# Decay sums of a selective scan: float32 products with a triangle, or broadcast bfloat16 weights over the triangle with the key's side as a bias

## The reference

```
dt = clip(softplus(dt + dt_bias), 0.001, 0.1);  A = -exp(A_log)
dA = min(exp(dt * A), 0.99)
h_t = clip(dA_t * h_{t-1} + x_t B_t^T, -10, 10)      # per sequence and head, 64 x 64
y_t = C_t h_t
```

## Time and profile before

| | |
|---|---|
| median of the runs | 1929.37 us (1928.33 to 1934.06) |
| profiled execution | 1936.8 us, its span 1934.7 us |
| the scan, first to last L2136 | 1684.13 to 1804.17 us, 120.04 us |
| TensorE busy there | 118.03 us, granted clock 1.00 |
| VectorE, ScalarE, GpSimd busy there | 102.05, 87.89 and 0.00 us |
| from there to the feed-forward | 12.61 us, granted clock 0.51 |

### The profile page before, as it was taken

The page is one execution under the profiler, slowest core; times in us unless marked ns, Lnnn a source line. Parts: engine busy times, 40 slices in busy tenths (PEclk is TensorE's granted clock), DMA queues, the critical chain, the costliest instruction groups (busy, mean ns, idle before and its releaser), DMA issues.

```text
span 1934.7 us, 41332 instructions
## 1 busy us (share of the span) xinstructions
PE 1749.8 (90%) x15442; PEld 659.6 (34%) x15442; DVE 1642.7 (85%) x2549; ACT 1522.6 (79%) x2881; POOL 459.9 (24%) x751
## 2 busy tenths in 40 slices
PE   7699999999999999999999999998996688899884
PEld 4232222222222222222222222226772344366552
DVE  7689999999999999999999999943345776588678
ACT  6469999999999999999999999993333567777454
POOL 2233210230001223222223222000006775000024
PEclk9799999999999999999999999999997899899787
DMA  3412222111101111111111111015765453423311
GB/s 119 158 63 88 75 66 66 53 56 41 30 28 41 51 41 46 53 40 43 56 42 42 53 45 56 10 39 158 211 173 156 110 143 104 134 61 88 93 62 33
DMA packets 156350, 146.36 MB, mean 76 GB/s; under 512 B 39882, under 2 KB 135117, under 8 KB 156002
## 3 DMA queue, kind: packets, MB, share of 16 engines
q1 hardware_dynamic: 147688, 126.17, 22.1%
q0 software_dynamic: 8352, 17.29, 3.3%
q10 hardware_dynamic: 122, 0.39, 0.1%
HBM read 80.80 MB, written 60.03 MB: 73 GB/s over the span
## 4 chain that ended last, share of the span: by engine, by line
PE 73%; ACT 9%; POOL 6%; issue 5%; DVE 4%; DMA 2%; ACTq 0%; SPq 0%; POOLq 0%; DVEq 0%
PE PS L1870 28%; PE PS L1896 16%; PE PS L1854 10%; POOL VP L1728 6%; ACT probs L1263 4%; PE PS L1943 4%; ACT SG L1252 2%; PE PS L2138 2%; PE PS L2120 1%; PE PS L1930 1%; PE PS L1816 1%; PE PS L2210 1%; PE PS L2141 1%; PE PS L2123 1%; PE PS L1922 1%
## 5 line engine op out<-in xcount | busy, mean ns | idle before, releaser
L812 DVE TENSOR_REDUCE mxp<-PS 128x1 f32<-128x1024 f32 x1024 | 1171.9, 1214 | 34.9 <-PE PS L1854 31.3
L1263 ACT ACTIVATE probs<-PS 128x512 f32<-128x512 f32 x2048 | 1095.9, 596 | 59.3 <-PE PS L1896 11.5
L1870 PE MATMUL PS<-probs,VH 128*32 128x256 f32 x8192 | 655.5, 392 | 35.4 <-ACT probs L1263 21.2
L1896 PE MATMUL PS<-stacks 51*128 51x512 bf16 x2048 | 414.5, 387 | 2.1 <-DVE mxp L812 1.1
L1854 PE MATMUL PS<-stacks 48*128 48x512 bf16 x2048 | 403.9, 380 | 13.3 <-DMA stacks<-kl_d 12.8
L1870 PEld LDWEIGHTS PS<-probs,VH 128*32 128x32 f32 x8192 | 162.3, 108 | 468.6 <-ACT probs L1263 239.7
L1896 PEld LDWEIGHTS PS<-stacks 51*128 51x128 bf16 x2048 | 109.9, 93 | 427.3 <-ACT probs L1263 393.1
L1728 POOL DMA_INDIRECT VP<-oe_d,ROWI x128 | 134.1, 1048 | 217.7 <-DMA oe_d<-stacks 174.1
L1620 POOL DMA_INDIRECT xe_d<-xn_s,rows_s x128 | 126.4, 988 | 214.9 <-PE PS L1870 181.6
L1598 POOL CAST spl<-nmx 128x8 bf16<-128x8 f32 x64 | 12.0, 188 | 514.3 <-DVE nmx L807 300.9
L826 DVE TENSOR_TENSOR stacks<-stacks,PS 128x640 f32<-128x640 f32 x32 | 26.3, 821 | 112.6 <-ACT stacks L1304 112.6
(11 more groups left out here) (358 smaller groups left out, 1809.4 us busy)
## 6 DMA issues: line engine op xcount, KB each, us to landing
xe_d<-zt SPq DMA_DIRECT2D x16, 640.0 KB
stacks<-xe_d SPq DMA_DIRECT2D x32, 320.0 KB, 3.7
oe_d<-stacks SPq DMA_DIRECT2D x32, 320.0 KB, 2.8
o_d<-SG SPq DMA_DIRECT2D x256, 32.0 KB, 1.9
ews<-in_ew_dram SPq DMA_DIRECT2D x33, 192.0 KB, 2.4
stacks<-ql_d SPq DMA_DIRECT2D x64, 96.0 KB
stacks<-kl_d SPq DMA_DIRECT2D x62, 96.0 KB
probs<-xs_d SPq DMA_DIRECT2D x18, 256.0 KB, 3.7
```

What stands on the lines that cost most here:

```text
L812: v.tensor_reduce(mxp[:, n // 2, n % 2:n % 2 + 1], MXB[n % 2].rearrange("p a c -> p (a c)"), X_AX, ALU.max).then_inc(mx_done, 1)
L1263: act.activation(probs[:, at:at + 512], PS[:, bank_of(u, e), :], ACT.Exp, scale=float(1.0 / np.sqrt(np.float32(DK)))).then_inc(exp_done, 1)
L1870: mm = pe.matmul(OB[32 * jg:32 * jg + 32, c:c + 256], VH[w][:, kt, :], probs[:, at:at + 256], start=(kt < 2 and half == 0), stop=(kt >= TC ...
L1896: pe.matmul(PS[:, bank_of(u, e), :], KS[w][o:o + KROWS + 3, kt * P:(kt + 1) * P], QS[w][o:o + KROWS + 3, q0:q0 + 512], start=True, stop=Tr ...
```

## The change

The exponent of a pair is no longer computed as one sum over the tokens between s and t. The running sums are made on their own, and the two sides of the pair meet in the exponential.

The decays are cut into three bfloat16 numbers whose sum is the float32 value (`la3`, once, before the scan). For each pair and each of the three parts, TensorE takes one column of them, repeated 128 times with step 0, as 128x128 weights over the triangle in bfloat16: `L_t`, the same in all 128 partitions. The key's side, `-L_s`, is one number for each partition: three matmuls before the scan give it for all chunks (bank 7), and ScalarE adds it as the bias of the exponential, one instruction for each pair. Above the diagonal the exponent is then positive, so VectorE bounds it by 1 before it multiplies with the triangle. `E2` is read from the same two banks, so bank 7 isn't used in the loop.

GpSimd takes over the squares of x, the turned bfloat16 copy of `E2` (now from `E2`, not a second exponential) and that of `DM`. VectorE's `spread_decays` is gone; its product into `DM` now waits for GpSimd's copy of the last `DM`.

```
+        la3 = spare[:, 0:3 * NT * NH1 // 2].bitcast(BF16).rearrange("p (k t h) -> p k t h", k=3, h=NH1)
+        tri16 = spare[:, 256:256 + P // 2].bitcast(BF16)
...
             def chunk_operands(c):
                 w = c % 2
-                if c + 1 < TCH:
-                    spread_decays(c + 1)
                 v.wait_ge(d_done, c + 1)
-                v.tensor_tensor(DM, DE, TRI.unsqueeze(1).broadcast_to([P, B * NH1, P]), ALU.mult).then_inc(dm_done, 1)
+                after(v, opb_ready, c)
+                v.scalar_tensor_tensor(DM, DE, 1.0, TRI.unsqueeze(1).broadcast_to([P, B * NH1, P]), ALU.min, ALU.mult).then_inc(dm_done, 1)
...
-            spread_decays(0)
+            link(v.tensor_copy(tri16, TRI))
+            link(v.tensor_copy(la3[:, 0], d0))
+            link(v.tensor_tensor(la_rest, d0, la3[:, 0], ALU.subtract))
+            link(v.tensor_copy(la3[:, 1], la_rest))
+            v.tensor_tensor(la3[:, 2], la_rest, la3[:, 1], ALU.subtract).then_inc(la_set, 1)
...
+            v.wait_ge(la_ready, 1)
+            v.tensor_scalar(d2, PS[:, 7, 0:NT * NH1].rearrange("p (t h) -> p t h", h=NH1), -1.0, None, ALU.mult).then_inc(la_set, 1)
...
             def chunk_exps(c):
                 w = c % 2
-                act.wait_ge(la_ready, c + 1)
+                act.wait_ge(la_ready, c + 2)
                 after(act, ops_ready, c)
-                act.activation(DE, PS[:, 0:2, :].rearrange("p b (h t) -> p (b h) t", h=NH1), ACT.Exp).then_inc(d_done, 1)
+                for b in range(B):
+                    for h in range(NH1):
+                        ins = act.activation(DE[:, b * NH1 + h, :], PS[:, b, h * P:(h + 1) * P], ACT.Exp,
+                                             bias=dtt[:, 1, b * TCH + c, h:h + 1])
+                ins.then_inc(d_done, 1)
                 after(act, hs_done, c - 1)
-                sums = by_head(PS[:, 7, :])
-                act.activation(E2[w], sums, ACT.Exp)
-                act.activation(E2b[w][:, :, 1:P], sums[:, :, 0:P - 1], ACT.Exp)
-                act.activation(E2b[w][:, :, 0:1], sums[:, :, P - 1:P], ACT.Exp).then_inc(el_done, 1)
+                for b in range(B):
+                    ins = act.activation(E2[w][rows_of(b), :, :], by_head(PS[rows_of(b), b, :]), ACT.Exp)
+                ins.then_inc(el_done, 1)
                 act.wait_ge(tile_ld[c % 4], TILE_BASE + 96 * (c // 4 + 1))
-                act.activation(RB[w][:, :, :, 0:HP], XS[c % 4].rearrange("p (b h n) -> p b h n", b=B, h=NH1), ACT.Square)
                 for b in range(B):
-                    act.activation(RB[w][:, b, :, HP:P], BS[c % 4][:, b, :].unsqueeze(1).broadcast_to([P, NH1, DS]), ACT.Square)
-                act.wait_ge(dm_done, c + 1)
-                act.activation(DMb[w][:, :, 1:P], DM[:, :, 0:P - 1], ACT.Copy)
-                act.activation(DMb[w][:, :, 0:1], DM[:, :, P - 1:P], ACT.Copy).then_inc(opb_ready, 1)
+                    ins = act.activation(RB[w][:, b, :, HP:P], BS[c % 4][:, b, :].unsqueeze(1).broadcast_to([P, NH1, DS]), ACT.Square)
+                ins.then_inc(sq_done, 1)
...
+            for c in range(TCH):
+                w = c % 2
+                pool.wait_ge(tile_ld[c % 4], TILE_BASE + 96 * (c // 4 + 1))
+                after(pool, c_done, c - 1)
+                xs = XS[c % 4].rearrange("p (b h n) -> p b h n", b=B, h=NH1)
+                for b in range(B):
+                    pool.tensor_tensor(RB[w][:, b, :, 0:HP], xs[:, b], xs[:, b], ALU.mult)
+                pool.wait_ge(el_done, c + 1)
+                pool.tensor_copy(E2b[w][:, :, 1:P], E2[w][:, :, 0:P - 1])
+                pool.tensor_copy(E2b[w][:, :, 0:1], E2[w][:, :, P - 1:P])
+                pool.wait_ge(dm_done, c + 1)
+                pool.tensor_copy(DMb[w][:, :, 1:P], DM[:, :, 0:P - 1])
+                pool.tensor_copy(DMb[w][:, :, 0:1], DM[:, :, P - 1:P]).then_inc(opb_ready, 1)
...
             def chunk_sums(c):
-                pe.wait_ge(lb_set, c + 1)
-                after(pe, d_done, c)
-                scaled = lb.rearrange("p (b h) t -> p b (h t)", b=B)
-                for b in range(B):
-                    pe.matmul(PS[:, b, :], BELOW, scaled[:, b, :], start=True, stop=True)
                 after(pe, el_done, c)
                 for b in range(B):
-                    mm = pe.matmul(PS[rows_of(b), 7, :], onesq[:, 0:DS], scaled[:, b, :], start=True, stop=True)
+                    for h in range(NH1):
+                        for k in range(3):
+                            mm = pe.matmul(PS[:, b, h * P:(h + 1) * P], la3[:, k, b * TCH + c, h:h + 1].broadcast_to([P, P]), tri16,
+                                           start=(h == 0 and k == 0), stop=(h == NH1 - 1 and k == 2))
                 mm.then_inc(la_ready, 1)
...
                 pe.wait_ge(opb_ready, c + 1)
+                pe.wait_ge(sq_done, SQ_BASE + c + 1)
...
+            pe.wait_ge(la_set, 1)
+            for k in range(3):
+                mm = pe.matmul(PS[:, 7, 0:NT * NH1], tri16, la3[:, k].rearrange("p t h -> p (t h)"), start=(k == 0), stop=(k == 2))
+            mm.then_inc(la_ready, 1)
             chunk_sums(0)
```

More of the change, by code:

```diff
@@ L236, in build @@
         sc_aff = sb("sc_aff", [P, 3, DI])
-        lb, DE, DM, MM0 = (VP[:, 8 * i:8 * i + 8, :] for i in range(4))
+        DE, DM, MM0 = (VP[:, 8 * i:8 * i + 8, :] for i in range(1, 4))
+        spare = VP[:, 0:8, :].rearrange("p t c -> p (t c)")
+        la3 = spare[:, 0:3 * NT * NH1 // 2].bitcast(BF16).rearrange("p (k t h) -> p k t h", k=3, h=NH1)
+        tri16 = spare[:, 256:256 + P // 2].bitcast(BF16)
+        la_rest = spare[:, 512:512 + NT * NH1].rearrange("p (t h) -> p t h", h=NH1)
         MM = [MM0, YM[:, 0:8, :]]
@@ L250, in build @@
         BD = [heads(t) for t in (probs[:, 3072:3584], ym_flat[:, 2048:2560])]
-        ldc = sb("ldc", [P, B, NH1])
         HS = sb("HS", [P, NH1, HP])
@@ L337, in build @@
         tile_ld = [sem(f"tile_ld{i}") for i in range(4)]
-        lb_set, la_ready, gg_set, d_done, el_done, dm_done, opb_ready, vr_out, ops_ready, c_done, y_out, hs_done = (
-            sem(n) for n in ("lb_set", "la_ready", "gg_set", "d_done", "el_done", "dm_done", "opb_ready", "vr_out", "ops_ready", "c_done", "y_out", "hs_done"))
+        la_set, la_ready, gg_set, d_done, el_done, dm_done, opb_ready, vr_out, ops_ready, c_done, y_out, hs_done = (
+            sem(n) for n in ("la_set", "la_ready", "gg_set", "d_done", "el_done", "dm_done", "opb_ready", "vr_out", "ops_ready", "c_done", "y_out", "hs_done"))
         bnd_read, yc_ready = sem("bnd_read"), sem("yc_ready")
+        sq_done, SQ_BASE = exp_out, 4
         okv = sb("okv", [P, 1])
@@ L1480, in chunk_out @@
                     act.activation(VR[b * DS:b * DS + 1, :, :], PS[0:1, 5 + b, :].rearrange("p (h t) -> p h t", h=NH1), ACT.Copy).then_inc(vr_out, 1)
+            act.wait_ge(la_set, 2)
             chunk_exps(0)
```

## The result

The changed kernel takes 1938.55 us (median of 20 runs, 1931.72 to 1953.87); the kernel before, run beside it, 1931.57 us (20 runs). The ratio is 1.0045, interval [1.003, 1.006]: slower by 7 us in medians, where 13.5 us less were forecast. The profiled execution took 1943.99 us.

The account below looks back on a forecast made before the run. TensorE's 8.09 us a chunk was taken to bound the scan. Fifteen chunks at 7.1 us give 106.5 us against 120.0, so -13.5 us from the median of 1929.4: 1916 us, range 1909 to 1929.

Parts of the forecast that it names:

- The rule on the clock: TensorE in the scan: its clock falls only after idling 2 us and more; expected gaps are under 0.5 us.
- rival E: TensorE idles a little each period and its clock falls: 5.17 + 1.66 us double to 13.7 us; chance 0.02.
- The collision: In the scan, GpSimd's casts delay VectorE's two-SBUF-input work, chiefly L1015: 0.27 us taken, making 7.1 us a chunk.
- Start at 0, bound +2: First chunk: second sums may run at 1.2 GHz after TensorE idles 2.6 us, at most +2 us; 0 taken.
- Part 1: Sums on TensorE: 24 bfloat16 matmuls at 0.069 us, 1.66 us a chunk, replace 2.92 us.
- Rival C: Step-0 weights load slowly on TensorE: 0.121 us a matmul, 8.07 us a chunk, 1929 to 1930 us; chance 0.08.
- Part 2 and 3: ScalarE: eight exponentials for DE, 2.2 us, hidden behind TensorE; VectorE: no decay spread, product into DM 1.23 us.
- rival B: ScalarE's DE is late: 7.2 us a chunk without collisions, 7.7 with them; 1919 to 1925 us; chance 0.15.
- Part 4: GpSimd in the scan: squares and casts sum to 3.5 us a chunk, half the period, with exclusion against VectorE.
- rival D: GpSimd with the exclusion becomes the bound: 8.9 us a chunk with dear casts, 1941 us; chance 0.12.
- 6.83 us loop: Scan: TensorE's products, then VectorE's four operations renewing the state; sums can shrink 1.26 us before this ends last.
- Rival A: Nothing collides in the scan: 6.83 us a chunk, 102.5 us, kernel 1908 to 1912 us; chance 0.13.

Follow-up runs that it names:

- e1: Changed kernel plus 12 useless bfloat16 matmuls a chunk on TensorE, ahead of the wait for the new state: 1927.77 us, ratio to before 0.9978.
- e8: Changed kernel without GpSimd's part; squares of x, `E2b` and `DMb` on ScalarE as before: ratio to before 1.0093.
- e2: Changed kernel with GpSimd's squares of x held until VectorE has renewed the state two chunks before: 1917.9 us, ratio to before 0.9936.
- e3: Changed kernel with the squares of x back on ScalarE, so GpSimd only copies: 1920.3 us, ratio to before 0.9941.
- e7: Changed kernel with only 60 useless matmuls added before the second sums: ratio to before 1.0025.
- e12: Changed kernel plus 6 useless matmuls a chunk in TensorE's idle time: ratio to before 1.0004.
- e5: e2 plus 40 useless matmuls between first and second sums and an early exponential loading ScalarE's table: ratio to before 0.9956.
- e6: e5 plus the state's first product before VectorE's wait for `DE`, and 34 useless matmuls before the last chunk's products: ratio to before 0.9927.
- e10: e6 run again on another chip: ratio to before 0.9941.
- e11: Kernel before with only GpSimd's part of the change, plus 14 useless float32 matmuls around the second sums: ratio to before 1.0036.

## Why the prediction was wrong

The trace of before had a sign of it, outside the scan. First two rows of its windows, then TensorE between them, then the window behind:

```profile
1870.00:1878.00 8.00, 8.00 (x33) 4.10 (x32) 7.40 (x32) 4.41 (x9) 0.00 (x0) 1.00 0.01 3
1878.00:1880.00 2.00, 1.42 (x11) 1.23 (x11) 1.90 (x12) 2.00 (x6) 0.00 (x0) 0.90 0.00 0
...
1879.12 5.13 PE L2198 MATMUL PS<-wff,waq 128*128 128x128 f32 x29 [0.58 <-DVE wff L1096]
...
1880.00:1882.00 2.00, 2.00 (x11) 2.00 (x11) 1.68 (x3) 1.97 (x3) 0.00 (x0) 0.50 0.32 93
```

TensorE was busy for 8.00 us without a break, idled once for 0.58 us, and its clock fell. Another fall of that trace, at about 121.8 us, had waits of 0.48, 0.69 and 1.08 us before it.

- **The rule on the clock failed**, rival E, which had 0.02. The step reads: "it fell here only after idling 2 us and more, and the gaps expected are under 0.5 us". The first half holds for the scan of before, where TensorE hardly waited at all; for the whole trace it is false, as the rows above show. The second half failed too: the gaps were 0.81 us, and behind the first chunk the clock fell three times, over four long periods. In the profiled scan 129.66 - (14 x 7.50 + 6.86) = 17.8 us are lost to it: 3.8 in the first chunk and 14.0 in the later ones. Over the 20 runs of the changed kernel time and mean granted clock go together at a correlation of -0.96 (0.940 with 1953.87 us, 0.953 with 1931.72 us): how long the clock is down differs from run to run. The Trainium skill (TensorE: Matmul & The Clock Gate, Part 1) says that "the default state is throttled, and activity releases the throttle". The runs agree in kind: useless activity alone took the ratio from 1.0045 to 0.9978 (e1).
- **The collision was mis-sized**: 0.27 us expected, 0.64 found. Its kind was right, its place wrong. I set GpSimd's casts beside the product with C; they fall beside L1002 (1.16 us instead of 0.75), where VectorE has time. What costs are the squares, which I put "in front of the casts" without asking when their wait, `c_done`, ends: just as VectorE's two products on the loop begin. 14 x (7.5 - 7.1) = 5.6 us; with the 17.8 us of the clock, and 0.2 less for the last period, that is the whole distance from 106.5 to 129.66 us.
- **Start at 0, bound +2**: the first chunk cost 3.8 us. ScalarE's table load (1.28 us) comes behind its wait for the first sums, and the exponentials for which the second sums wait take 3.2 us behind it (1674.68 to 1677.90); TensorE idles 3.78 us where 2.6 were expected, and not only the second sums but the chunk is slow. How much of this belongs to the change is open: e1 and e8 idle there for 3.78 and 4.86 us, and their first chunks ran at full clock (7.97 and 7.45 us). The first L2149 came 2.0 us earlier than the 1684.1 expected. The chance that chunk 15 keeps the clock did not come either.
- **Part 1 held**: 24 matmuls of step-0 weights take 1.51 us from first start to last end against 1.66, 0.060 us each. Rival C is out, and what the prediction took from the Trainium skill on the column step (TensorE: Matmul & The Clock Gate, Weight-path perf modes) agrees with this.
- **Part 2 and 3 held**: 2.17 against 2.2 us, 1.23 against 1.23. ScalarE ended nothing at full clock; rival B is out.
- **Part 4's work held**: casts 0.67 + 0.39 + 1.23 + 0.21 and squares 1.18 undisturbed, 3.7 us against 3.5. So rival D, the only one on the slower side with a chance that counted, is out: GpSimd was far from being the bound. The sign was right by another mechanism.
- **The 6.83 us loop of the prediction was right**: e2 and e3 show it at 6.86, and with it the scan is 12.6 us shorter than before. Rival A is the changed kernel without its one collision.

## What to carry to other kernels

When a change shortens TensorE's part of a loop, work out how long it then waits in each period, and don't take the shortened loop at full clock unless the trace shows such a loop, and look for falls in the whole trace and not only in the stretch that changes: here waits of 0.81 us in 7.50 lost 14.0 us behind the first chunk, more than the 14 x 0.6 us that the shorter period had gained, and both ways out (close the gap, or fill it with useless matmuls) paid. When work goes to GpSimd, ask for each instruction at which event it starts and what VectorE does then; moving it behind the next semaphore (here `hs_done`) can be worth more than the move itself. Read the granted clock of each stretch before reading busy shares.

## What the runs showed of the hardware

- Falls to 1.2 GHz came in loops with waits of 0.81 us a period (after, e7) and of 0.25 to 1.46 us (e8), once behind a single wait of 0.58 us (before, at 1879 us), and not in loops with 0.04, 0.18 and 0.37 us (e1, e2, e12). They came in some periods and not in others of equal form; what picks them is open.
- In the loop the fall shows behind the gap: the product right behind it ran at full speed (0.69 us), the next did not (2.80 and 3.68 us). Full clock ahead of a gap of 1.84 to 3.26 us did not save the chunk behind it (e5, e6, e7, e10, e11); behind gaps of 3.78 and 4.86 us with nothing in them the first chunk was fast in e1 and e8 and slow in the changed kernel and e2. The length of the gap alone does not say which.
- VectorE's product of two SBUF operands, 128x256, took 0.83 us beside GpSimd's instruction of two SBUF operands and 0.42 beside none; two others 3.54 instead of 0.75 us among five of GpSimd's; the reduction from PSUM stayed at 1.28 us beside GpSimd's squares.
- Eight exponentials of 128x128 with a bias by pointer take 2.17 us, 0.27 each; without one the second of a pair added 0.18 us.
